# A Mamba scan with a mixture of experts on one core: a third state bank, five banks in rotation, and sums of y joined by DMAs

## What is computed

```python
xn = _layernorm(x)
# branch s: a Mamba block, then an MLP with silu (both with a residual)
xz = rmsnorm(xn) @ in_proj_w.T ; xp, z = split(xz)           # 512 channels each
xc = silu(causal conv of 4 taps over xp)
dt, B, C = from xc (x_proj 16+16+16, dt_proj, softplus)      # 16 states per channel
h = h * exp(dt * A) + (dt * xc) * B_t ;  y_t = sum over the 16 states of h * C_t
y = (y + xc * D) * silu(z) ;  s = xn + y @ out_proj_w.T ;  s = s + silu(rmsnorm(s) @ w1.T) @ w2.T
# branch g: top 2 of 8 experts, each 256 -> 1024 -> 256
g = silu(sum over 2 experts of gate * (relu(xn @ w1[e] + b1[e]) @ w2[e] + b2[e]))
out = x + s * g
```

## Time and profile before

| | us |
|---|---|
| median of 3 runs (1599.95 to 1605.29) | 1604.46 |
| the profiled execution, its device time | 1611.44 |
| its span from the first to the last instruction | 1609.6 |
| PE busy / DVE busy / POOL busy / ACT busy | 1349.1 / 1258.5 / 1164.6 / 890.1 |
| PE's mean granted clock, share of full speed | 0.902 |

### The profile page before, as it was taken

How to read it: one execution, slowest core, us unless ns; L and a number is a source line. 1 busy time by engine, 2 the same in 40 slices (tenths; PEclk the granted TensorE clock), 3 DMA queues, 4 the chain that set the end, 5 groups by cost and what they waited for, 6 DMA issues and landing times.

```text
span 1609.6 us, 17492 instructions
## 1 busy us (share of the span) xinstructions
PE 1349.1 (84%) x5158; PEld 957.9 (60%) x5158; DVE 1258.5 (78%) x1571; ACT 890.1 (55%) x1948; POOL 1164.6 (72%) x590
## 2 busy tenths in 40 slices
PE   4874762988988998989998997899998998889977
PEld 2641211766676856766776666676776676646546
DVE  6689864778878986789887977889887987777734
ACT  4643352574756665576667565655756464545522
POOL 0535888867887778877896778776996789786730
PEclk8587766999999998999999998999998999979889
DMA  4774443655474637754474537464575457456540
GB/s 161 274 256 144 152 156 136 228 199 165 135 283 156 225 100 228 249 183 172 172 274 167 202 122 259 161 226 159 190 248 197 146 169 276 157 184 203 180 152 27
DMA packets 124607, 300.64 MB, mean 187 GB/s; under 512 B 14408, under 2 KB 29136, under 8 KB 114016
## 3 DMA queue, kind: packets, MB, share of 16 engines
q1 hardware_dynamic: 112224, 272.91, 49.9%
q0 software_dynamic: 6144, 16.79, 3.2%
q10 hardware_dynamic: 6144, 9.83, 1.7%
HBM read 259.75 MB, written 39.71 MB: 186 GB/s over the span
## 4 chain that ended last, share of the span: by engine, by line
PE 41%; DVE 14%; issue 13%; POOL 9%; ACT 8%; DMA 5%; SPq 1%; DVEq 0%; ACTq 0%; POOLq 0%
PE prod L944 33%; DVE state L1322 9%; DMA xs<-slot_x 4%; POOL dbu L681 4%; PE ysum L993 4%; POOL hxc L692 3%; DVE hxc L1290 2%; POOL slot_x L668 2%; PE prod L1128 1%; ACT state L752 1%; PE prod L949 1%; PE prod L1129 1%; ACT late L910 1%; DVE prod L1359 1%; DMA late<-slot_y,slots 1%
## 5 line engine op out<-in xcount | busy, mean ns | idle before, releaser
L1322 DVE TENSOR_TENSOR_SCAN state<-state,carry,dbu 128x512 f32<-128x512 f32 x512 | 657.7, 1285 | 179.1 <-ACT state L752 148.6
L681 POOL TENSOR_TENSOR dbu<-dtu,bb 128x1024 f32<-128x1024 f32 x256 | 608.1, 2383 | 67.3 <-DVE state L1322 58.4
L692 POOL TENSOR_TENSOR hxc<-hxc 128x1024 f32<-128x1024 f32 x155 | 366.5, 2364 | 223.9 <-DVE hxc L1290 223.9
L752 ACT ACTIVATE state<-dt,par 128x512 f32<-128x512 f32 x512 | 353.5, 692 | 94.3 <-DVE hxc L1290 78.1
L1290 DVE TENSOR_TENSOR hxc<-state,cb 128x512 f32<-128x512 f32 x512 | 353.7, 691 | 36.2 <-DVE state L1322 0.5
L944 PE MATMUL prod<-late 128*128 128x256 f32 x1136 | 281.6, 406 | 26.6 <-issue 17.0
L993 PE MATMUL ysum<-hxc,ident 128*128 128x512 f32 x404 | 224.8, 686 | 75.6 <-DVE hxc L1290 41.4
L944 PE MATMUL prod<-xsT,late 128*128 128x256 f32 (+1 forms) x1280 | 270.2, 365 | 15.7 <-DVE xc L1345 3.9
L944 PEld LDWEIGHTS prod<-late 128*128 128x128 f32 x1136 | 236.2, 211 | 71.2 <-issue 37.3
L944 PEld LDWEIGHTS prod<-xsT,late 128*128 128x128 f32 x1280 | 226.9, 196 | 68.8 <-issue 37.8
L750 ACT COPY carry<-state 128x1 f32<-128x1 f32 x384 | 61.1, 159 | 250.3 <-DVE hxc L1290 234.5
(11 more groups left out here) (164 smaller groups left out, 1216.7 us busy)
## 6 DMA issues: line engine op xcount, KB each, us to landing
bb<-bc_rows SPq DMA_DIRECT2D x256, 256.0 KB
cb<-bc_rows SPq DMA_DIRECT2D x256, 256.0 KB
late<-moe SPq DMA_DIRECT2D x40, 1028.0 KB, 4.9
late<-moe SPq DMA_DIRECT2D x40, 1024.0 KB, 5.8
slot_x<-xc SPq DMA_DIRECT2D x18, 512.0 KB, 5.7
xs<-slot_x SPq DMA_DIRECT2D x31, 256.0 KB, 6.1
slot_y<-ys ACTq DMA_DIRECT2D x31, 256.0 KB, 5.4
late<-x SPq DMA_DIRECT2D x12, 512.0 KB, 9.4
```

The source lines that it names most:

```text
L681: nc.gpsimd.tensor_tensor(dbu[:, v % 3, :, :], dtu[:, n % 2, 2 * h:2 * h + 2, :], b, ALU.mult).then_inc(dbu_ready, 1)
L692: nc.gpsimd.tensor_tensor(hxc[:, to, :, :], hxc[:, to, :, :], hxc[:, piece, :, :], ALU.add).then_inc(summed, 1)
L752: nc.scalar.activation(state[:, k % 2, :], dt[:, (2 * n + h) % 3, k % 2, :], ACT.Exp, scale=par[:, P_ALOG + col(k):P_ALOG + col(k) + 1]).t ...
L1322: nc.vector.tensor_tensor_scan(state[:, c, :], state[:, c, :], dbu[:, v % 3, c, :], carry[:, n % 2, col(k):col(k) + 1], ALU.mult, ALU.add) ...
```

## The change

The eight PSUM banks are dealt out anew. `state` gets three banks in place of two, so `decay(k)` waits for product k - 3. `ysum` is gone: `prod` has five banks, and sums of y that still go through PE (blocks 0 and 7) take two of the five for as long as the sum is open. In the middle no sum goes through PE. The four groups of a half form a chain (`Y_CHAIN`); when POOL has added up group 2, 3 or 4, it issues a DMA (`LINK`) that adds this group's buffer onto the first group's buffer in SBUF, 128x1024. `YE` reads the sum from `hxc`. Such halves are listed in `WHOLE`. `hxc` has 7 buffers, since the first group's is held for the whole half. On ACT the preparation of the next block stands one step later (`"A": 2`). There are 53 ACCs in place of 101, and 36 DMAs more.

```diff
-GROUPS = [((1,) * NS,) * 2] + [((4,) * 4,) * 2] * (NB - 2) + [((4,) * 3 + (1,) * 4, (2,) * 2 + (1,) * 12)]
-HX = 5
+ALONE = ((1,),)
+GROUPS = [(ALONE * NS,) * 2] + [(((4, 4, 4, 4),),) * 2] * (NB - 2) + [(((4,),) * 3 + ALONE * 4, ((2,),) * 2 + ALONE * 12)]
+HX = 7
+BANKS = 5
+STATES = 3
+MID_LATER = 0
...
-LATER = {"act": {"R": 1, "M": 1, "C": 1, "A": 1}, "dve": {"M": 1, "C": 1, "A": 0}, "pool": {"Y": 1, "A": 1},
...
+LATER = {"act": {"R": 1, "M": 1, "C": 1, "A": 2}, "dve": {"M": 1, "C": 1, "A": 0}, "pool": {"Y": 1, "A": 1},
...
+WHOLE = [r for r in LAST_GROUP if LAST_UNIT[LAST_GROUP[r]] - FIRST_UNIT[FIRST_GROUP[r]] == NS - 1]
...
-        free += [e for e in back if e[0] <= 2 * v + 99]
+        free += back
...
-            back.append((2 * v + 6, table[FIRST_UNIT[q]][0], ("y_acc", q + 1)))
+            r, place = Y_CHAIN[q]
+            if place:
+                back.append((2 * v + 9, table[FIRST_UNIT[q]][0], ("linked", q)))
+            if q == LAST_GROUP[r]:
+                back.append((2 * v + (14 if place else 6), table[FIRST_UNIT[FIRST_GROUP[r]]][0], ("y_acc", accs_until(r)) if r not in WHOLE else
+                             ("y_whole", 2 * WHOLE.index(r) + 2)))
...
-        if Y_UNIT[v][1] == Y_UNIT[v][2] - 1:
-            out[2 * v + 1].append(("Y", "ACC", Y_UNIT[v][0]))
+        q, j, n = Y_UNIT[v]
+        r, place = Y_CHAIN[q]
+        if j == n - 1 and place:
+            out[2 * v + 2].append(("Y", "LINK", q))
+        if j == n - 1 and q == LAST_GROUP[r] and r not in WHOLE:
+            out[2 * v + (6 if place else 1)].append(("Y", "ACC", r))
...
-    count, table, until = [0] * 4, {}, [(-99, b) for b in range(4)]
+    count, filled, table, until = [0] * BANKS, [0] * BANKS, {}, [(-99, b) for b in range(BANKS)]
...
+        elif kind == "Y" and name == "ACC" and FIRST_UNIT[FIRST_GROUP[i]] % NS == 0:
+            for c in range(2):
+                take(("Y", "SUM%d" % c, FIRST_UNIT[FIRST_GROUP[i]] // NS))
...
-        state = ctx.enter_context(nc.psum_tensor("state", [P, 2, BT], F32))
-        ysum = ctx.enter_context(nc.psum_tensor("ysum", [P, 2, BT], F32))
-        prod = ctx.enter_context(nc.psum_tensor("prod", [P, 4, BT], F32))
+        state = ctx.enter_context(nc.psum_tensor("state", [P, STATES, BT], F32))
+        prod = ctx.enter_context(nc.psum_tensor("prod", [P, BANKS, BT], F32))
...
+        def group_added(eng, q):
+
+            if Y_CHAIN[q][1]:
+                eng.wait_ge(linked[Y_CHAIN[q][0] % 4], 16 * links_until(q))
...
+                elif kind == "Y" and name == "LINK":
+                    group_summed(pool, i)
+                    group_added(pool, i - 1)
+                    to, piece = (HX_OF[FIRST_UNIT[q]][0] for q in (FIRST_GROUP[Y_CHAIN[i][0]], i))
+                    pool.dma_start(flat3(hxc[:, to, :, :]), flat3(hxc[:, piece, :, :]), accum_op=ALU.add
+                                   ).then_inc(linked[Y_CHAIN[i][0] % 4], 16)
...
-                if k >= 2:
-                    act.wait_ge(hc_ready, k - 1)
-                if 2 <= k < (NB - 2) * BASE_STEP + 2:
-                    b = (k - 2) // BASE_STEP % 2
-                    nc.scalar.copy(carry[:, b, col(k - 2):col(k - 2) + 1], state[:, k % 2, BT - 1:BT]).then_inc(carried, 1)
-                    act.wait_ge(carried, k - 1)
-                nc.scalar.activation(state[:, k % 2, :], dt[:, (2 * n + h) % 3, k % 2, :], ACT.Exp,
+                last = k - STATES
+                if last >= 0:
+                    act.wait_ge(hc_ready, last + 1)
+                if 0 <= last < (NB - 2) * BASE_STEP:
+                    b = last // BASE_STEP % 2
+                    nc.scalar.copy(carry[:, b, col(last):col(last) + 1], state[:, k % STATES, BT - 1:BT]).then_inc(carried, 1)
+                    act.wait_ge(carried, last + 1)
+                nc.scalar.activation(state[:, k % STATES, :], dt[:, (2 * n + h) % 3, k % 2, :], ACT.Exp,
                                      scale=par[:, P_ALOG + col(k):P_ALOG + col(k) + 1]).then_inc(decay_ready, 1)
...
-                    v = LAST_UNIT[i]
-                    first = FIRST_UNIT[i] % NS == 0
-                    if first and v >= NS:
-                        pe.wait_ge(y_free, 2 * (v // NS))
-                    if Y_UNIT[v][1]:
-                        pe.wait_ge(summed, adds_before(v) + 1)
+                    v, start = LAST_UNIT[LAST_GROUP[i]], FIRST_UNIT[FIRST_GROUP[i]]
+                    first = start % NS == 0
+                    sums = [("Y", "SUM%d" % c, v // NS) for c in range(2)]
+                    if first:
+                        free(pe, sums[0])
+                        free(pe, sums[1])
+                    if v > start:
+                        group_summed(pe, FIRST_GROUP[i])
+                        group_added(pe, LAST_GROUP[i])
                     else:
                         pe.wait_ge(hc_ready, 2 * v + 2)
                     for c in range(2):
-                        last = pe.matmul(ysum[:, c, :], ident[:, :], hxc[:, HX_OF[FIRST_UNIT[i]][0], c, :], start=first,
+                        last = pe.matmul(bank(sums[c]), ident[:, :], hxc[:, HX_OF[start][0], c, :], start=first,
                                          stop=v % NS == NS - 1)
                     last.then_inc(y_acc, 1)
...
+                    elif what and what[0] == "linked":
+                        group_added(dve, what[1])
+                    elif what and what[0] == "y_whole":
+                        dve.wait_ge(y_whole, what[1])
                     elif what:
                         dve.wait_ge(y_acc, what[1])
                 dve.wait_ge(scanned, k + 1)
-                nc.vector.tensor_tensor(hxc[:, buf, c, :], state[:, c, :], cb[:, v % 4, :],
+                nc.vector.tensor_tensor(hxc[:, buf, c, :], state[:, k % STATES, :], cb[:, v % 4, :],
                                         ALU.mult).then_inc(hc_ready, 1)
...
-                        dve.wait_ge(y_acc, Y_UNIT[(2 * i + c // 2) * NS + NS - 1][0] + 1)
+                        key = ("Y", "SUM%d" % (c % 2), 2 * i + c // 2)
+                        chain = Y_CHAIN[Y_UNIT[(2 * i + c // 2) * NS][0]][0]
+                        if chain in WHOLE:
+                            group_added(dve, LAST_GROUP[chain])
+                            y, taken = hxc[:, HX_OF[(2 * i + c // 2) * NS][0], c % 2, :], (y_whole, 1)
+                        else:
+                            dve.wait_ge(y_acc, accs_until(Y_CHAIN[Y_UNIT[(2 * i + c // 2) * NS + NS - 1][0]][0]))
+                            y, taken = bank(key), is_free(key)
                         nc.vector.scalar_tensor_tensor(out=xc[:, p, c, :], in0=xc[:, p, c, :],
-                                                       scalar=par[:, P_D + c:P_D + c + 1], in1=ysum[:, c % 2, :],
-                                                       op0=ALU.mult, op1=ALU.add).then_inc(y_free, 1)
+                                                       scalar=par[:, P_D + c:P_D + c + 1], in1=y,
+                                                       op0=ALU.mult, op1=ALU.add).then_inc(*taken)
...
-                        dve.wait_ge(y_free, i * DC + c + 1)
+                        chain = Y_CHAIN[Y_UNIT[(2 * i + c // 2) * NS][0]][0]
+                        if chain in WHOLE:
+                            dve.wait_ge(y_whole, 2 * WHOLE.index(chain) + c % 2 + 1)
+                        else:
+                            read_out(dve, ("Y", "SUM%d" % (c % 2), 2 * i + c // 2))
```

More of the change, by code:

```diff
@@ L228, in reader @@
         return "act", (kind, "DN%d" % (size(i) - 1), i)
+    if kind == "Y":
+        return "dve", ("C", "YE%d" % (i % 2 * 2 + int(name[3])), i // 2)
     if kind == "R" and name in ("LG", "BL"):
@@ L248, in take @@
         until.append((read, bank))
-        table[key] = (bank, count[bank])
+        table[key] = (bank, count[bank], filled[bank])
         count[bank] += 1
+        filled[bank] += key[0] != "Y"
     for kind, name, i in PROLOGUE + program("pe"):
@@ L382, in mamba_moe @@
         consts = sem("consts")
-        full_ = [sem("full%d" % i) for i in range(4)]
-        free_ = [sem("free%d" % i) for i in range(4)]
+        full_ = [sem("full%d" % i) for i in range(BANKS)]
+        free_ = [sem("free%d" % i) for i in range(BANKS)]
         x_in = [sem("x_in%d" % g) for g in range(NB)]
@@ L418, in mamba_moe @@
         summed = sem("summed")
+        linked = [sem("linked%d" % i) for i in range(4)]
         y_acc = sem("y_acc")
-        y_free = sem("y_free")
+        y_whole = sem("y_whole")
         x1_in = sem("x1_in")
@@ L756, in do @@
                 if kind == "S" and name == "FIRST":
-                    decay(0)
+                    for k in range(1):
+                        decay(k)
                 elif kind == "S":
```

38 lines of the change are left out of this document (24 added, 14 removed).

## The result

The changed kernel took 1576.56 us in the median of four runs (1572.70 to 1577.30), the kernel before 1602.50 us beside it (1599.95 to 1605.29). The ratio is 0.9831, with a 95% interval from 0.9810 to 0.9851: faster by 1.7%, 26 us, where 76 were forecast. The profiled execution took 1575.95 us, with a span of 1574.1 us.

The account below looks back on a forecast made before the run. The bound was taken to be engines waiting for each other, mainly DVE's scan for ACT's decay (118.4 us in blocks 1 to 6). Terms 75 + 15 - 24 + 10 gave 76 us gained, 1604.5 to 1528; range 1480 to 1585.

Parts of the forecast that it names:

- the likeliest case: Whole kernel: the forecast's own sum, 76 us gained, 1528 us, with terms varying inside 1500 to 1555; chance 0.57.
- rival 2: PE's backlog, through ACT's line, stays the pace: 34 us gained, 1570, or 1595 with YE's 24 us; chance 0.17.
- The third state bank: Blocks 1 to 6: decay may begin 1.98 us earlier, taking 75.4 of 118.4 us off DVE's 59 decay waits.
- PE without 48 ACCs: PE, blocks 1 to 6: 82 us less work makes ACT's copies earlier; 15 us gained, ends 0 and 43.
- YE reads SBUF: DVE, blocks 1 to 6: 24 YEs held by POOL's instructions, 24 us lost, ends 0 and 57.
- 36 DMAs on POOL: POOL, blocks 1 to 6: 36 us more work, covered by its 208.8 us idle before adds; counted 0.
- When the sum is ready: YE, blocks 1 to 6: a half's last DMA may take about 14 us before anyone waits; cost taken as 0.
- Rival 4: YE waits for its half's last DMA; each us beyond 14 costs 12, up to 1697 us; chance 0.09.
- The order on ACT: ACT: later preparation costs the state bank's lead in the convolution; no gain counted in DVE's 20.5 us of tanh waits.
- Blocks 0 and 7: First and last block: fewer decay waits (4 and 12 us), 6 us against block 7; 10 us gained, ends -10 and 20.
- Rival 5: POOL's inputs dbu come late and blocks 0 and 7 lose on three banks: 36 + 20 us lost, 1585; chance 0.05.
- the one for rival 2: Sign in the changed profile: DVE's waits for ACT's decay in blocks 1 to 6 stay over 60 us.

Follow-up runs that it names:

- e15: Changed kernel with all its work, but POOL waits, two steps ahead of its turn, until both YE of a half are done: 1534.49 us, 0.9598.
- e9: Changed kernel, but YE in blocks 1 to 6 reads a PSUM state bank in place of the joined sum, which is left out: 1531.39 us, 0.9511.
- e4: Changed kernel with two state banks and ACT's order of before; DMAs that add and YE from SBUF stay: 1603.95 us, 1.0001.
- e13: Changed kernel with POOL waiting one step ahead for both YE, two state banks and ACT's order of before: 1575.75 us, 0.9857.
- e14: Changed kernel with POOL waiting one step ahead for both YE, three state banks, ACT's order of before: 1547.60 us, 0.9681.
- e3: Changed kernel with PE summing every group again (48 ACCs, no DMAs that add), three state banks, sums taking two of five product banks: 1648.20 us, 1.0305.
- e8: Changed kernel with four product banks in place of five, one PSUM bank unused: 1597.30 us, 0.9940.
- e7: Kernel before, but YE in blocks 1 to 6 takes its second input from a constant SBUF tile, leaving out the sum of y: 1639.57 us, 1.0223.
- e12: Changed kernel with the experts' weights loaded only once; the 78 later 1 MB loads and PE's waits for them left out: 1574.04 us, 0.9795.
- e5: Changed kernel, but SP loads the experts' rows earlier, ahead of the next first weights: 1573.40 us, 0.9792.
- e16: The kernel of e15 with the experts' rows loaded early, by the edit of e5: 1534.10 us, 0.9580.
- e1: Changed kernel, but YE in blocks 1 to 6 leaves out the sum of y, so it has one SBUF input: 1566.56 us, 0.9794.

## Why the forecast was right in sign and 50 us off in size

The range held the time, and the likeliest case was the wrong one: 1576 lies near what rival 2 gives, 1570 and 1595. That nearness is chance in good part. Rival 2 allows 34 us of gain before YE's cost, and the kernels in which YE is hardly held gained 64 to 68 us (e15) and 71 to 78 (e9). Point by point, in the forecast's order:

*The third state bank, 75 us.* This is the step that failed most: "each of the 59 waits can lose at most that much", 1.98 us, was taken for what each loses. The decay waits of the middle fell by 63 us (118.4 to 55.1), but 25 of them went by the rest of the change and 38 by the bank with ACT's order (e4). Without much of a lock the bank alone took 28 (e13 to e14). What was taken off these waits did come off the end: 28 us of waits and 28 us of time from e13 to e14, and 38 us less YE's 9 for 27 us of time from e4 to the change. So it is the waits that don't shrink by the lead. The forecast had named the reason as a possibility, a lead that is not rebuilt: ACT's waits for PE before `ys` were 57.4 us with two banks and 73.1 with three (e13, e14), and e3 shows it at its worst, with three state banks and still 116.5 us of decay waits. That is the reasoning of rival 2. That ACT hands the wait on is read from these rows and was not measured by itself; other waits of ACT for PE went down (before `xpad`, 27.2 us before and 4.2 in the changed kernel, where the preparation stands a step later).

*PE without 48 ACCs, 15 us.* About right, with a term missing: the forecast had no price for the fifth bank, which is worth 17 us (e8, with the lock and three state banks). e13 has the ACCs gone and the banks given to products, but not the third state; it is 23 us faster than before, with 7 us of YE's delay still in it, so this part with blocks 0 and 7 is worth 30 us where the forecast had 25. PE's busy time in the middle fell by 58 us, not by 80 to 100. The ACCs' rows are gone (96.6 us of busy time before, 3.0 now), but the rows of PE's other matmuls add up to 933 us where they made 909, at a granted clock of 0.93 for 0.95, which the forecast expected to stay. That PE would give less than it loses in work was right.

*YE reads SBUF, 24 us: the second step that failed.* "Meets one with a chance of 0.85 and has half of it left" is wrong in its second half. Five YEs did not get in when the POOL instruction that they met ended, but waited for the next one too, and the next, through four at 807.38. 46 us were added to DVE's instructions, near the upper end of 57, and they cost 36 us in the kernel before (e7) and 45 to 51 in the changed one (e9). The two small rows at the earlier trace rows could not show this: POOL had one instruction there, and nothing behind it. The other 14 that met POOL were held for 1.2 to 2.3 us only, as the forecast had it. Six halves look like this one, in which POOL had waited just before:

```profile
898.89 1.21 DVE L1420 SCALAR_TENSOR_TENSOR xc<-xc,par,hxc 128x512 f32<-128x512 f32 x1
900.02 0.68 DVE L1350 TENSOR_TENSOR hxc<-state,cb 128x512 f32<-128x512 f32 x1
900.62 2.29 DVE L1420 SCALAR_TENSOR_TENSOR xc<-xc,par,hxc 128x512 f32<-128x512 f32 x1
...
897.20 2.35 POOL L737 TENSOR_TENSOR hxc<-hxc 128x1024 f32<-128x1024 f32 x1 [0.89 <-DVE hxc L1350]
899.51 2.85 POOL L726 TENSOR_TENSOR dbu<-dtu,bb 128x1024 f32<-128x1024 f32 x1
```

Here YE did get in: the first one ended at 900.10, 0.55 us after POOL's add (899.55), although POOL's next instruction follows at 899.51 without a wait. That one took 2.85 us, 0.5 more than the add. The same is seen at seven other YEs, two of which (986.89 and 989.01) stand in a half where POOL had not waited just before. So who is let in at the end of a POOL instruction isn't settled by these rows; all that were held through several stood behind a POOL that had worked without a gap. The price then hangs on how far POOL is behind DVE, and not on POOL's busy share alone. It also grows when DVE is less held up elsewhere: in e12 other waits shrank and YE's 24 lines took 85.8 us. The Trainium skill (SBUF — State Buffer, Who interferes with whom) says that whoever issues first gets the shared ports for its whole instruction and the other blocks fully. The eight YEs agree with that; the five don't, if the order of issue is the order of the rows' starts, since YE's row at 807.38 starts before POOL's rows at 808.82, 811.13 and 813.42. The measurement decides.

*36 DMAs on POOL, 0 us.* Right: 0.81 us each in the median, and POOL still had 163.6 us before its adds. *When the sum is ready, 0 us.* Right: the transfers landed after 5.0 to 10.3 us, inside the 14 allowed, and one YE waited, for 2.9 us, at 1153.90; POOL, behind by then, had issued its DMA only at 1144.00. Rival 4 is out:

```profile
L743 POOL DMA_DIRECT2D hxc<-hxc x36: 694/813/1037, 322.2 to 1317.7; - x36
...
  DVE xc L1420: 2.9, 1
...
DMA to landing us min/median/max: 5.0/7.9/10.3
```

*The order on ACT, 0 us.* Wrong: the preparation one step later was worth 6 to 13 us (e14). *Blocks 0 and 7, 10 us.* Right, 8 came, with 6 us of YE's delay in the stretch of block 7. *Rival 5* is half of what happened, with the roles the other way round: POOL was hardly late (DVE's waits for `dbu` rose from 4.1 us to 11.4), it held DVE. Of the signs, the one for rival 2 did not show: the decay waits stayed under 60 us, at 55.1, though not at 30.

The sum again, forecast against runs: PE, buffers and blocks 0 and 7 25 against 30 (e13 and its 7 us of YE), bank and order 75 against 41, YE -24 against -45. That is 76 against 26. The runs' terms are from several series and good to a few us each, so that they meet the 26 exactly is luck. Of the 50 us that are missing, 34 are the bank's term, 21 to 27 the lock's, and the rest gives 5 back. Without the lock term the forecast's sum would have been 100 us gained, 1504; the run that takes the lock out (e9) gave 1531.

What stays open: the 49 to 56 us of decay waits that are left in e9 and e15, with some 75 us of ACT before `ys`. The experts' rows don't set them (57.9 us in e5, 54.3 in e16). Their weights take part (34.6 us in e12, against 55.1), and so do product banks (65.4 in e8); how much time the weights are worth without the lock was not tried. What decides whether a held YE gets in between two POOL instructions stays open too. Nor did a run separate, in the lock's 45 to 51 us, DVE's delay from the lengthening of POOL's own instructions.

## What to carry to other kernels

Before moving an operand of a VectorE instruction from PSUM to SBUF, look at whether GpSimd works without a gap at that moment: the price can be a whole row of its instructions, not the rest of one (32 of the 46 us here came from five such cases). If the operand must be in SBUF and GpSimd has idle time, let GpSimd wait for the VectorE instruction; here that one wait turned 26 us of gain into some 64. A buffer more gives each wait a lead, but the waits need not shrink by it, since the engine that runs ahead meets its next wait sooner; test with the one resource put back (two state banks: 28 us, 27 to 41 with the order on ACT, where the list said 75).

## What the runs showed of the hardware that was not expected

- A VectorE instruction held by GpSimd was in some cases not let in between back-to-back GpSimd instructions: 9.13 us through four of them, and 10.74 us through five in e12, ended 0.56 us after the last. In eight other cases of the changed kernel it was let in at the end of the first, and GpSimd's next instruction took longer.
- In f32 a `tensor_scalar` with a single SBUF input, 128x512, is held too: 470/1605/9805 ns as minimum, median and maximum of 24 (e1). The section of the Trainium skill named above says that `tensor_scalar` can enter a mode with two ports and then contends; its fastest instance, 470 ns beside 721 for the form with a PSUM input, fits that.
- The lock works the other way too: behind the YE that ended at 900.10, POOL's next instruction, started at 899.51, took 2.85 us where that line's mean is 2.44.
- A DMA of 512 KB that adds in SBUF landed after 5.0/7.9/10.3 us, beside the 3.2 us that the forecast had estimated from the Trainium skill (DMA: Bandwidth & Descriptors, Anatomy of one DMA) for a plain one. The measured time is the one to use.
